# Cross attention on one Trainium2 core: the value works of batch 14 move to every second cycle

## The reference, cut to what matters

```python
Q = relu(x @ Wq + bq); K = relu(ctx @ Wk + bk); V = relu(ctx @ Wv + bv)
scores = einsum('hbqd,hbkd->hbqk', Qh, Kh) / sqrt(8)      # 16 heads
scores = where(key_mask == 0, NEG, scores)                # rows of ctx that sum to 0
attn = softmax(scores) * q_mask
out = einsum('hbqk,hbkd->hbqd', attn, Vh) + x
```

## Time and profile before

| | |
|---|---|
| Time, median of 3 runs | 355.78 us (355.68 to 355.84) |
| Time of the profiled execution | 355.85 us |
| Its span, first to last instruction | 354.1 us |
| Mean granted TensorE clock | 0.996 |
| Busy: TensorE matmul, ScalarE, VectorE | 98%, 85%, 67% |

### The profile page before, as it was taken

How to read it: one execution, slowest core, us unless ns; L and a number is a source line. 1 busy time by engine, 2 the same in 40 slices (tenths; PEclk the granted TensorE clock), 3 DMA queues, 4 the chain that set the end, 5 groups by cost and what they waited for, 6 DMA issues and landing times.

```text
span 354.1 us, 16749 instructions
## 1 busy us (share of the span) xinstructions
PE 345.4 (98%) x6698; PEld 235.4 (66%) x6698; DVE 236.4 (67%) x777; ACT 299.3 (85%) x395; POOL 4.4 (1%) x28
## 2 busy tenths in 40 slices
PE   8899999999999999999999999999999999999994
PEld 4565676776757677675767767576676767667662
DVE  4789487775848577484857848486784848679321
ACT  1587789888898988889898888989889898989993
POOL 4000000000000000000000000000000000000000
PEclk9999999999999999999999999999999999999998
DMA  7678757777854747385464738547473754537100
GB/s 233 219 250 293 215 190 236 262 231 229 293 136 180 209 156 224 91 292 135 177 203 158 231 91 291 137 169 213 152 236 91 282 147 171 177 111 238 11 10 8
DMA packets 41667, 65.29 MB, mean 184 GB/s; under 512 B 28197, under 2 KB 30758, under 8 KB 41638
## 3 DMA queue, kind: packets, MB, share of 16 engines
q1 hardware_dynamic: 40418, 64.09, 56.3%
q10 hardware_dynamic: 1220, 0.80, 0.8%
HBM read 13.67 MB, written 0.82 MB: 41 GB/s over the span
## 4 chain that ended last, share of the span: by engine, by line
PE 93%; DMA 2%; DVE 2%; issue 1%; ACTq 1%; ACT 1%
PE psum L694 40%; PE psum L670 29%; PE psum L614 12%; PE psum L605 11%; DMA bq_sb<-in_bq 2%; PE psum L785 1%; DVE values L951 1%; ACT probs L568 0%; DVE k_low L922 0%; DVE v_biased L941 0%; ACTq L513 0%; PE psum L793 0%; ACT queryT L526 0%; ACTq L515 0%; DVE flat_mask L1109 0%
## 5 line engine op out<-in xcount | busy, mean ns | idle before, releaser
L568 ACT ACTIVATE probs<-psum 121x800 f32<-121x800 f32 x384 | 293.2, 840 | 37.6 <-PE psum L670 37.6
L694 PE MATMUL psum<-probs,values 121*17 121x200 f32 x3072 | 154.8, 334 | 0.0
L670 PEld LDWEIGHTS psum<-query_bd,k_parts 64*121 64x121 f32 x1536 | 91.7, 181 | 50.8 <-ACT probs L568 35.0
L670 PE MATMUL psum<-query_bd,k_parts 64*121 64x200 f32 x1536 | 115.5, 281 | 0.3 <-ACT probs L568 0.2
L694 PEld LDWEIGHTS psum<-probs,values 121*17 121x17 f32 x3072 | 78.0, 97 | 41.3 <-issue 1.7
L898 DVE TENSOR_SCALAR_CACHE_REDUCE k_raw<-psum,bk_sb 128x361 f32<-128x361 f32 (+2 forms) x63 | 37.2, 592 | 53.3 <-PE psum L605 53.2
L614 PE MATMUL psum<-wv_sb,keyT 128*32 128x129 f32 (+1 forms) x1536 | 53.8, 273 | 0.1
L605 PE MATMUL psum<-keyT,wk_mixed 128*32 128x361 f32 (+2 forms) x504 | 51.2, 481 | 1.0 <-DVE flat_mask L1109 0.6
L614 PEld LDWEIGHTS psum<-wv_sb,keyT 128*32 128x32 f32 (+1 forms) x1536 | 43.7, 108 | 6.4 <-DVE v_biased L941 0.5
L951 DVE TENSOR_SCALAR values<-v_biased,keep 121x128 f32<-121x128 f32 x192 | 43.3, 283 | 6.1
L941 DVE TENSOR_TENSOR v_biased<-psum,bv_sb 121x384 f32<-121x384 f32 x64 | 35.0, 548 | 0.0
(11 more groups left out here) (77 smaller groups left out, 63.8 us busy)
## 6 DMA issues: line engine op xcount, KB each, us to landing
k_parts<-k_high SPq DMA_DIRECT2D x30, 722.0 KB, 4.8
k_parts<-k_low SPq DMA_DIRECT2D x30, 722.0 KB, 5.5
keyT<-in_ctxT SPq DMA_DIRECT2D x15, 722.0 KB, 4.3
query_rep<-late_high SPq DMA_DIRECT2D x2, 600.0 KB, 3.8
query_rep<-late_low SPq DMA_DIRECT2D x2, 600.0 KB, 4.2
residual<-in_x SPq DMA_DIRECT2D x64, 12.5 KB
out<-residual SPq DMA_DIRECT2D x60, 12.5 KB
k_parts<-k_high SPq DMA_DIRECT2D x2, 359.0 KB, 3.4
```

The costliest lines, as they stand in the source:

```text
L568: nc.scalar.activation(probs[0:KTILE, u % PROB_SLOTS], scores_ps[0:KTILE, u % SCORE_SLOTS, :, 0:QCOLS], ACT.Exp, scale=SCALE).then_inc(pro ...
L670: mm = nc.tensor.matmul(scores_ps[0:KTILE, u % SCORE_SLOTS, j, n * TCOLS:(n + 1) * TCOLS], k_parts[rows, parity, t, kt * KTILE:(kt + 1) * ...
L694: mm = nc.tensor.matmul(spans[c * VCOLS:c * VCOLS + VUSED, half, :, :, 0:SPAN], values[0:KTILE, parity, kt, half * HALF_PAIRS + c, 0:VUSED ...
```

## The change

In batch 14 only (`keys=False`), the four value works stand in cycles 0, 2, 4 and 6 in place of 0 to 3. A cycle with a value work does the products of two units and leaves the third to the next cycle, which does four. VectorE's queue follows: `spread_queries` stands ahead of the read of the last value work (g = 3) in place of behind it. Number, size and order of the matmuls of each kind are the same.

```diff
+            LATE_WORK = {2 * g: work for g, work in enumerate(VALUES)}
+            LATE_ENDS = [cycle * CYCLE + (CYCLE if cycle not in LATE_WORK else CYCLE - 1) for cycle in range(CYCLES)]
+            LATE_PRODUCTS = [range(start, end) for start, end in zip([0] + LATE_ENDS, LATE_ENDS)]
+            assert LATE_ENDS[-1] == UNITS
@@ TensorE, batch()
-                    for u in units:
-                        value_products(b, parity, u)
-                    k, ahead = SIDE_WORK[cycle]
+                    if last or keys:
+                        for u in units:
+                            value_products(b, parity, u)
+                    else:
+                        for u in LATE_PRODUCTS[cycle]:
+                            value_products(b, parity, u)
+                    k, ahead = LATE_WORK.get(cycle, (0, AFTER)) if not keys else SIDE_WORK[cycle]
@@ VectorE, batch()
                 for g in range(VGROUPS):
+                    if g == VGROUPS - 1 and not keys:
+                        spread_queries(b + 1, 1 - parity)
                     finish_values(b + 1, 1 - parity, g, used + g)
@@
-                spread_queries(b + 1, 1 - parity)
+                if keys:
+                    spread_queries(b + 1, 1 - parity)
                 finish_keep(b + 1, 1 - parity)
```

## The result

The changed kernel takes 356.58 us (median of 22 executions, 355.6 to 360.05), the kernel before 355.62 us (22 executions beside it). The ratio is 1.0032, 95% interval 1.0017 to 1.0047: slower, by 0.6 to 1.7 us, about 0.96 us by the medians. The forecast was 356.65 us, with a chance of 0.6 of being slower. The profiled execution took 356.58 us, its span is 354.8 us.

A forecast was written before the change was run, and what follows sets the result against it. TensorE was taken to bound the kernel overall, ScalarE behind 324.04. ScalarE's 0.5 us won, then VectorE's chain delaying batch 15's products, summed to +0.87: 355.78 + 0.87 = 356.65 us, range 355.9 to 357.1.

The forecast's parts named there:

- The hand-over and TensorE's sum: Batch 14: TensorE bounds up to 324.04, ScalarE behind it; even cycles 2.23 us, odd ones 2.34 plus 0.2 of waiting.
- the margin of 0.08 us: Odd cycles of batch 14: TensorE reaches its third scores 0.08 us before ScalarE is done, so it waits.
- the 0.6 taken: Three odd-cycle waits ahead of cycle 6 of batch 14, charged 0.2 us each; 0.6 us taken, bounds 0 to 0.9.
- VectorE's queue: From the read of value work 3, 3.65 us of VectorE's work precede batch 14's output turn; batch 15's first product 0.80 late.
- The sum of +0.87 us: Whole change: the exponential of unit 6 of batch 15 starts at 335.85, a loss of 0.87 us; bounds +0.2 to +1.2.
- The 0.5 us won for ScalarE: Start of batch 15: its first exponential at 330.1 against 330.6, 0.5 us earlier (1.1 without the waits).
- the rival in which VectorE is in time: Batch 14's output turn starts when the products end, so ScalarE keeps its 0.5 us: 355.2 us; chance 0.05.
- 1.0 us to spare: Low keys' transfers, issued at 322.5, land at 328.6, 1.0 us ahead of burst 7, batch 15's first scores.
- my own signs of being wrong: Three signs: L979 starts as the products end, odd cycles show no wait, or burst 7 waits for DMA.
- the rival of the late keys: Low keys or queries late, landing over 6.5 us, hold burst 7: +1.2 to +2, 357 to 357.8 us; chance 0.05.
- No wait in the odd cycles: Batch 14's odd cycles have no waits, so the loss is only +0.2 to +0.7: 356.0 to 356.5 us; chance 0.32.
- The falling clock: TensorE's clock falls in its new wait of 1 us ahead of batch 15's products: 358.3 us or more; chance 0.03.

The follow-up runs named there:

- e1: The changed kernel with bound_scores and sum_heads moved from ahead of batch 14's turn to behind the second half of the low keys; 355.82 us, ratio 0.9992.
- e3: The changed kernel with VectorE's maximum over 1600 columns done twice; 359.86 us, ratio 1.0106 to the kernel before.
- e4: The kernel before the change with VectorE's maximum over 1600 columns done twice; 355.63 us, ratio 0.9983.
- e7: The changed kernel with only both halves of the low keys put behind value work 0, so their transfers are issued earlier; 356.38 us, ratio 1.0016.
- e2: The changed kernel with bound_scores and sum_heads moved earlier and both halves of the low keys behind value work 0; 355.41 us, ratio 0.9984.
- e8: The changed kernel with the passed-on product put between the second and third unit of scores in odd cycles; 356.84 us, ratio 1.0022.
- e9: The changed kernel with spread_queries back behind the read of value work 3, leaving only TensorE's part; 358.82 us, ratio 1.0106.

## Why the prediction was right

**The hand-over and TensorE's sum.** Even cycles 2.28 us (predicted 2.23), odd ones 2.52, 2.45 and 2.44 (2.34 + 0.2). The third scores of odd cycles waited, as the margin of 0.08 us said; against an odd cycle of 2.28 us without waits the three cost 0.24, 0.17 and 0.16, together 0.57 of the 0.6 taken. Burst 7 would have started 16.52 us behind the first (327.06 + 2.28 - 312.82), predicted 16.52; the errors of the two kinds of cycle cancelled, which was luck. Value work 3 was read 16.66 us behind it, predicted 16.66.

**VectorE's queue.** 3.65 us from that read to the turn, predicted 3.65. From there TensorE's first product took 0.81 (0.76 and 0.05 for the weights), the products 1.14 and the exponential 0.50. The sum of +0.87 us stands against +0.85 in the traces and +0.96 in the medians. That this chain is the cause is shown by e1, which takes it away and with it the loss, by e3 and e4, which lengthen it and pay only after the change, and by e7.

**The gain.** The 0.5 us won for ScalarE is there in e2: its burst 7 starts at 329.16 - 312.65 = 16.51 us, 17.02 before. My price for the rival in which VectorE is in time, 355.2, was too low by about 0.5 us: e1, which is that case, gains 0.02 us in the stage and not 0.5. There are two reasons. The low keys hold burst 7, which is 0.26 us of the stage (e2 against e1). And the passed-on product is paid for in cycle 7, which delays the burst behind it; that is the rest, and it is left in e2.

**What I had wrong.** I gave the low keys 1.0 us to spare. Their transfers were issued when I said (322.3 against 322.5), but the cover was not there. The trace after, last part of the chain of work:

```profile
322.87 6.87 DMA k_parts<-k_low
```

I had taken the median of two landings, 5.5 us, for the later of the two. In the trace before these two transfers took 3.9 and 7.1 us, so the later one was never at 5.5; counted with 7.1, it lands at 330.2, behind the 329.6 that I had for burst 7. After the change it took 6.87, and burst 7 waited 0.37. So the last of my own signs of being wrong, burst 7 waiting for DMA, was there, and the rival of the late keys, to which I gave 0.05, happened in its mechanism. It came out at neither its price of +1.2 to +2 nor one for one on top of the sum. VectorE's chain starts from value work 3, which is filled ahead of that wait, and the turn was later still (e7). That it cost the total nothing was luck; once VectorE is in time it costs 0.26 us of the stage (e1 against e2).

ScalarE idled 0.71 us ahead of unit 6, not 1.3: burst 7 was late by the low keys and with it the six exponentials ahead of the idle time (e7, without that wait: 0.99), and the last of the six ends 0.84 us after its start, where I had counted 0.73. The total does not depend on this.

**The rivals.** No wait in the odd cycles: refuted by 1.05 in place of 0.81. The Trainium skill ("TensorE: Matmul & The Clock Gate", Step-by-step: what each phase is for) has weight loads pulled ahead of matmuls in flight. Had that held across a wait, the sum would by my estimate be 0.4 us lower; the stage doesn't bear that out. The row of PEld at the wait of 326.38, before the change, shows the load itself:

```profile
326.38 0.29 PEld L670 LDWEIGHTS psum<-query_bd,k_parts 64*121 64x121 f32 x4 [0.40 <-ACT probs L568]
```

It starts with its matmul and not ahead of it: the load was not pulled ahead of the wait. The same holds for the first products behind the new wait (load at 333.90, product at 333.94). But the 0.12 that I charged for this had too narrow a reason, as e8 shows: a unit of scores that stands alone behind a product, with no wait, took 0.39 as well, and there too the load starts with its matmul (321.06). So 0.39 is the cost of a unit that opens a burst anew, whatever broke the burst. And the unit to compare it with is the third of an unbroken burst, not the mean: at 323.53 before the change it starts at 324.04 and takes 0.30 us, so the wait adds 0.09 and not 0.12.

The falling clock: not in the changed kernel's profile, but real, at a wait of 2.8 us.

**Open.** Two of the 22 executions of the changed kernel took 359.73 and 360.05 us at a mean clock of 0.987. The kernel before has such executions too (359.6 at 0.988), so they say nothing of the change, and without a trace their place is unknown.

## What to carry to other kernels

When work is moved later on the bounding engine, follow what consumes it: here an engine with 3.90 us of idle had the rest of its queue pushed behind the moved work, and the copy that the next batch waits for stood last in that queue. Put work that doesn't need the late arrival ahead of it in the queue, and not behind it. For a group of transfers that one consumer waits for, take the last landing, not the median.

## What the runs showed of the hardware

- Matmuls of one kind in a row are cheaper than their mean: scores of 8, 12 records take 0.60, 0.81 us to the next kind, so 0.21 per unit and 0.18 per burst; four alone take 0.39, as this sum says (e8).
- After a wait of TensorE of 2.77 us the granted clock averaged 0.57 over the next 4 us (e3); after one of 2.69 us it stayed at 1.00 in the profiled execution (e9), and after 0.84 us in the changed kernel too.
- Two transfers of 722 KB each, issued 0.6 us apart, landed 3.9 and 7.1 us behind their issue before the change, 5.8 and 6.87 us after it.
